# Transposes of the next element ahead of its loop turn, the last query tile in halves, row sums spread, and layer 1's values on VectorE

## The reference

```
layer 0:  deg = sum(adj, -1);  agg = adj @ x / max(deg, 1e-6);  relu(concat(x, agg) @ W.T)
layer 1:  Xw = X @ Wv + bv;  sj = Xw @ aw[:d];  si = Xw @ aw[d:]
          alpha = A * exp(leaky_relu(sj[None, :] + si[:, None] + ab, 0.2))
          T = alpha / (sum(alpha, -1) + 1e-12)
          H = sum_k (T^k X) @ Wk[k] + bk[k]   (k = 0, 1, 2);   relu(H)
layer 2:  three graph convolutions adj @ (x @ W) + b, relu after the first two
layer 3:  attention, 8 heads of 32: softmax(q k^T * scale * (adj + adj)) v, then @ Wo + bo
```

## Time and profile before

| | us |
|---|---|
| median of 3 runs (lowest, highest) | 3148.42 (3145.50, 3149.03) |
| the profiled execution | 3147.59 |
| its span, first to last instruction | 3145.7 |
| TensorE busy (matmul) | 3023.7 |
| VectorE busy | 2083.8 |
| ScalarE busy | 1724.0 |

### The profile page before, as it was taken

The page is one execution under the profiler, slowest core; times in us unless marked ns, Lnnn a source line. Parts: engine busy times, 40 slices in busy tenths (PEclk is TensorE's granted clock), DMA queues, the critical chain, the costliest instruction groups (busy, mean ns, idle before and its releaser), DMA issues.

```text
span 3145.7 us, 71077 instructions
## 1 busy us (share of the span) xinstructions
PE 3023.7 (96%) x28188; PEld 2644.0 (84%) x28188; DVE 2083.8 (66%) x4020; ACT 1724.0 (55%) x3048; POOL 453.5 (14%) x1666
## 2 busy tenths in 40 slices
PE   6999999999999999999999999999999999999999
PEld 6988789887898778987789877898778987789877
DVE  5637976379762797627975289753887438874387
ACT  3525854258552684426844278542784327853377
POOL 0101211012110122101221012111121111211112
PEclk9999999999999999999999999999999999999999
DMA  5122131121321213202133021330213302133110
GB/s 218 36 72 69 45 145 54 57 70 45 142 77 37 66 52 135 90 28 66 49 135 108 11 72 42 135 108 14 68 51 125 108 14 72 50 124 108 28 39 19
DMA packets 145271, 234.50 MB, mean 75 GB/s; under 512 B 12840, under 2 KB 113965, under 8 KB 144941
## 3 DMA queue, kind: packets, MB, share of 16 engines
q1 hardware_dynamic: 144940, 229.96, 22.5%
HBM read 120.86 MB, written 83.89 MB: 65 GB/s over the span
## 4 chain that ended last, share of the span: by engine, by line
PE 80%; DVE 10%; ACT 3%; issue 2%; SPq 2%; POOL 2%; DMA 0%; DVEq 0%; POOLq 0%; ACTq 0%
PE ps L725 15%; PE ps L497 15%; PE ps L499 14%; PE ps L498 14%; PE ps L715 9%; PE ps L743 7%; DVE rsum L1280 2%; PE ps L598 2%; SPq L400 1%; PE ps L587 1%; PE ps L756 1%; DVE ev L1379 1%; PE ps L555 1%; DVE t_lo L1210 1%; POOL rstd L461 1%
## 5 line engine op out<-in xcount | busy, mean ns | idle before, releaser
L1466 DVE CUSTOM_DVE_ANT_0 r<-ps,adjn 128x1024 f32<-128x1024 f32 x512 | 620.7, 1212 | 19.5 <-DVE xr L1502 10.3
L1141 ACT ACTIVATE r<-r,nmax 128x1024 f32<-128x1024 f32 x512 | 584.9, 1142 | 23.0 <-POOL nmax L489 22.6
L497 PE MATMUL ps<-u_hi,t_hi 128*128 128x256 f32 x2048 | 589.9, 288 | 5.8 <-DVE u_lo L1190 4.8
L499 PE MATMUL ps<-u_hi,t_lo 128*128 128x256 f32 x2048 | 579.2, 283 | 0.0
L498 PE MATMUL ps<-u_lo,t_hi 128*128 128x256 f32 x2048 | 578.8, 283 | 0.0
L725 PEld LDWEIGHTS ps<-ident,r 128*128 128x128 f32 x4096 | 462.5, 141 | 115.4 <-issue 77.6
L725 PE MATMUL ps<-ident,r 128*128 128x128 f32 x4096 | 536.7, 274 | 7.3 <-DVE pt L1482 6.9
L1482 DVE COPY pt<-ps 128x512 f32<-128x512 f32 x512 | 352.9, 689 | 92.6 <-PE ps L725 75.0
L497 PEld LDWEIGHTS ps<-u_hi,t_hi 128*128 128x128 f32 x2048 | 391.2, 191 | 14.3 <-DVE t_lo L1190 7.7
L907 ACT ACTIVATE pt<-ps 128x512 f32<-128x512 f32 x512 | 304.0, 594 | 175.8 <-PE ps L725 161.9
L498 PEld LDWEIGHTS ps<-u_lo,t_hi 128*128 128x128 f32 x2048 | 391.1, 191 | 0.0
(11 more groups left out here) (162 smaller groups left out, 5233.9 us busy)
## 6 DMA issues: line engine op xcount, KB each, us to landing
adjn<-in_adj SPq DMA_DIRECT2D x64, 512.0 KB, 3.4
t_spill<-t_hi SPq DMA_DIRECT2D x64, 512.0 KB, 4.5
t_spill<-t_lo SPq DMA_DIRECT2D x64, 512.0 KB, 5.3
t_hi<-t_spill SPq DMA_DIRECT2D x32, 1024.0 KB, 5.3
t_lo<-t_spill SPq DMA_DIRECT2D x32, 1024.0 KB, 8.0
xn<-in_x SPq DMA_DIRECT2D x16, 512.0 KB, 4.5
x_spill<-xn SPq DMA_DIRECT2D x64, 128.0 KB, 1.7
q_stack<-u_hi SPq DMA_DIRECT2D x64, 128.0 KB, 2.4
```

Source lines behind the costliest of these rows:

```text
L497: pe.matmul(dst, a_hi, b_hi, start=first, stop=False, skip_group_check=check)
L499: return pe.matmul(dst, a_lo, b_hi, start=False, stop=last, skip_group_check=check)
L1141: act.activation(r[:, s % RSLOTS, :], r[:, s % RSLOTS, :], ACT.Exp, bias=nmax[:, s % 4:s % 4 + 1], accum_out=prow[:, qt % 2, h:h + 1]).the ...
L1466: dve.tensor_tensor_reduce(out=r[:, s % RSLOTS, :], in0=ps[:, 2 * (s % 2):2 * (s % 2) + 2, :].rearrange("p a c -> p (a c)"), in1=adjn[:, q ...
```

## The change

What it does, in the order of an element:

- **Drain.** For elements after the first, TensorE transposes the first halves of adj column blocks 0 and 1 at stage UNITS + 1 and of 2 and 3 at UNITS + 5, inside the previous element's loop; ScalarE and VectorE take them out there, and VectorE makes the first row sum there. For element 0 the four stand ahead of the loop. The order of units in layer 0 and of the g products is new (one g pair behind each adj block).
- **Last query tile.** The spread moves from stage UNITS + 4 to UNITS + 2, rbc ahead of tile 6's normalisation; the last context product goes to bank 0; c_f, c_hi, c_lo of this tile are made in two halves of 128 columns, and the output product takes them one by one.
- **Row sums.** One in the drain, three ahead of tile 0, four behind tiles 0 to 3.
- **Layer 1.** `s_j` half 0 is taken out by ScalarE (a copy with a bias), all four `v` pairs by `both_rows` on VectorE; v pair 0 goes ahead of the late transposes, pair 3 ahead of the first hop; the last three `s_i` move later, with a scratch output elsewhere.
- **Layer 1's row product.** Own parts are issued two tiles ahead.

The diff, cut to its core:

```diff
-    TP_L0 = adj_units(0, 1) + x_units(0, 0) + adj_units(2, 3) + x_units(0, 1) + adj_units(4, 5, 6, 7)
+    TP_L0 = ([("adj", j, half) for half in range(HALVES) for j in range(TPH)] + x_units(0, 0) + adj_units(4, 5) +
+             x_units(0, 1) + adj_units(6, 7))
...
-            return ((4, 5, 2, 3)[n % 4],)
+            return (2 + n % 4,)
...
-                [("sj", 0), ("v", 0), ("v", 1), ("sj", 1), ("v", 2), ("v", 3)] +
+                [("sj", 0), ("v", 0), ("v", 1), ("v", 2), ("sj", 1), ("v", 3)] +
...
+        def ctx_bank(grp):
+
+            return ACC if grp == 2 * NT - 1 else 6
...
             pe.wait_ge(set_act, 13)
+            for j in range(TPH):
+                transpose_adj(0, j, 0)
             for b in range(B):
 
-                transpose_adj(b, 0, 0)
-                transpose_adj(b, 0, 1)
+                for j in range(TPH):
+                    transpose_adj(b, j, 1)
                 transpose_x_half(b, 0, 0)
-                transpose_adj(b, 0, 2)
-                transpose_adj(b, 0, 3)
+                transpose_adj(b, 4, 0)
+                transpose_adj(b, 4, 1)
                 pe.wait_ge(drained, b + 1)
-                project_pairs(b, "g", W_L0G, xt_wait(b, 0), range(2))
+                project_pairs(b, "g", W_L0G, xt_wait(b, 0), range(1))
+                transpose_adj(b, 5, 0)
+                transpose_adj(b, 5, 1)
+                project_pairs(b, "g", W_L0G, xt_wait(b, 0), range(1, 2))
                 transpose_x_half(b, 0, 1)
-                transpose_adj(b, 0, 4)
-                transpose_adj(b, 0, 5)
-                project_pairs(b, "g", W_L0G, xt_wait(b, 0), range(2, PAIRS))
-                transpose_adj(b, 0, 6)
-                transpose_adj(b, 0, 7)
+                transpose_adj(b, 6, 0)
+                transpose_adj(b, 6, 1)
+                project_pairs(b, "g", W_L0G, xt_wait(b, 0), range(2, 3))
+                transpose_adj(b, 7, 0)
+                transpose_adj(b, 7, 1)
+                project_pairs(b, "g", W_L0G, xt_wait(b, 0), range(3, PAIRS))
...
                 s_j(b, 0)
+                project_pairs(b, "v", W_K2, xt_wait(b, 1), range(1))
                 transpose_x_late(b, 1, 1)
-                project_pairs(b, "v", W_K2, xt_wait(b, 1), range(1))
+                project_pairs(b, "v", W_K2, xt_wait(b, 1), range(1, 2))
                 transpose_x_late(b, 1, 2)
-                project_pairs(b, "v", W_K2, xt_wait(b, 1), range(1, 2))
+                project_pairs(b, "v", W_K2, xt_wait(b, 1), range(2, 3))
                 s_j(b, 1)
                 transpose_alpha(b, 0, 0)
-                project_pairs(b, "v", W_K2, xt_wait(b, 1), range(2, 3))
+                project_pairs(b, "v", W_K2, xt_wait(b, 1), range(3, 4))
...
-                project_pairs(b, "v", W_K2, xt_wait(b, 1), range(3, 4))
                 transpose_alpha(b, 1, 0)
...
+                own_part = lambda t: project(pr_bank(b, pr["h", t])[:, 0:F], W_K0, t).then_inc(pr_full, 1)
+                own_part(0)
+                own_part(1)
                 for t in range(NT):
-                    project(pr_bank(b, pr["h", t])[:, 0:F], W_K0, t).then_inc(pr_full, 1)
                     row_product(b, t, AF_P2)
+                    if t + 2 < NT:
+                        own_part(t + 2)
...
+                    if s in (UNITS + 1, UNITS + 5) and b + 1 < B:
+                        for j in ((0, 1) if s == UNITS + 1 else (2, 3)):
+                            transpose_adj(b + 1, j, 0)
+                    if s >= 12 and (s - 12) % H == 0 and (s - 12) // H < NT - 1:
                         spread_denominators(b, (s - 12) // H)
+                    if s == UNITS + 2:
+                        spread_denominators(b, NT - 1)
...
+                act.activation(sj_row[:, 0:512], ps[:, PR + pr["sj", 0] % 2, :], ACT.Identity,
+                               bias=e_const[:, 0:1]).then_inc(sj_act, 1)
                 x_late_transposed(b, 1, 1)
                 normalise(b, 0, NT - 1)
...
-                rows_from_pr(b, "v", range(2, 3))
...
-                rows_from_pr(b, "v", range(3, PAIRS))
...
+                    if s >= 21 and (s - 21) % H == 0 and (s - 21) // H < NT and s != UNITS + 5:
                         normalise(b, 3, (s - 21) // H)
+                    if s == UNITS + 8:
+                        normalise(b, 3, NT - 2)
...
+                    if s >= 13 and (s - 13) % H == 0 and (s - 13) // H < NT - 1 or s == UNITS + 3:
+                        qt = NT - 1 if s == UNITS + 3 else (s - 13) // H
...
+                            copy(c_hi[:, 0, :], c_f[:, 0, :]).then_inc(c_hi_ready, 1)
+                            act.wait_ge(c_raw, nth(b, NT + 1, NT + 1))
+                            copy(c_hi[:, 1, :], c_f[:, 1, :]).then_inc(c_hi_ready, 1)
+                    if s in (UNITS + 2, UNITS + 7) and b + 1 < B:
+                        adj_transposed(b + 1, (0, 1) if s == UNITS + 2 else (2, 3), (0,))
...
+                dve.wait_ge(xr_free, b + 1)
+                rows_from_pr(b, "g", U_G, range(3, PAIRS))
+                degree(b, range(1, TPH))
+                inverse_degrees(b, 0)
...
+                    if t < TPH:
+                        degree(b, (TPH + t,))
+                    if t == TPH - 1:
+                        inverse_degrees(b, 1)
+                        dve.wait_ge(deg_ready, nth(b, 3, 2))
+                    if 2 <= t < NT - 1:
                         s_i(b, t - 2)
...
-                s_j(0)
-                s_i(b, NT - 2)
+                both_rows(0)
                 x_late_transposed(b, 1, 1)
-                both_rows(0)
+                both_rows(1)
                 x_late_transposed(b, 1, 2)
                 weights(0, 0)
-                both_rows(1)
-                s_i(b, NT - 1)
+                both_rows(2)
                 weights(0, 1)
-                s_j(1)
+                s_j()
                 al_transposed(0, 0)
-                rows_from_pr(b, "v", U_V - 2, range(2, 3))
+                s_i(b, NT - 3)
+                both_rows(3)
                 weights(0, 2)
...
+                    if s == UNITS + 2 and b + 1 < B:
+                        adj_transposed(b + 1, (0, 1), (0,))
+                        degree(b + 1, (0,))
+                    if s == UNITS + 8 and b + 1 < B:
+                        adj_transposed(b + 1, (2,), (0,))
...
+                    if s == UNITS + 6:
+                        dve.wait_ge(rbc_ready, nth(b, NT, NT))
+                        for g in range(2):
+                            dve.wait_ge(ctx_done, nth(b, 2 * NT, 2 * NT - 1 + g))
+                            dve.tensor_tensor(c_f[:, g, :], ps[:, ctx_bank(2 * NT - 2 + g), g * P:(g + 1) * P], rbc[:, g, :],
+                                              ALU.mult).then_inc(c_raw, 1)
+                        for g in range(2):
+                            dve.wait_ge(c_hi_ready, nth(b, NT + 1, NT + g))
+                            rest(c_lo[:, g, :], c_f[:, g, :], c_hi[:, g, :], c_ready)
...
                         if qt == NT - 1:
                             dve.sem_inc(drained, 1)
+                            if b + 1 < B:
+                                adj_transposed(b + 1, (3,), (0,))
```

More of the change, by code:

```diff
@@ L134, in build_program @@
             t_lo = sb("t_lo", [P, NT, N], F32R, s)
+        with ExitStack() as s:
+            t_cols = sb("t_cols", [P, N - F], F32, s)
+            si_out = sb("si_out", [P, F], F32, s)
         with ExitStack() as s:
@@ L301, in tp_x, with adj_freed @@
             return tp["x", layer, half, 0]
[L303 to L305 removed]
+        def adj_freed(j):
+            return tp["adj", j, HALVES - 1] + 1
         def x_ready(layer, rows):
@@ L576, in transpose_x_late, with transpose_adj @@
                     last.then_inc(tp_full, 1)
[L578 to L589 removed]
+            def transpose_adj(b, j, half):
+                n = tp["adj", j, half]
+                tp_wait(b, n)
+                for t in range(TPH):
+                    i = TPH * half + t
+                    if j == 0:
+                        pe.wait_ge(adj_in[i], nth(b, 16, 16))
+                    last = pe.transpose(tp_bank(n)[:, t * P:(t + 1) * P], adjn[:, i, j * P:(j + 1) * P], ident)
+                last.then_inc(tp_full, 1)
             def transpose_alpha(b, part, t):
@@ L950, in x_late_transposed, with adj_transposed @@
                     copy(dst, src).then_inc(tp_hi, 1)
-            def adj_transposed(b, layer, j):
-                for half in range(HALVES):
-                    n = tp_a(layer, j) + half
-                    act.wait_ge(tp_full, nth(b, TP_UNITS, n + 1))
-                    copy(t_hi[:, j, half * 512:(half + 1) * 512], tp_bank(n)).then_inc(tp_hi, 1)
+            def adj_transposed(b, js, halves=range(HALVES)):
+                for j in js:
+                    for half in halves:
+                        n = tp["adj", j, half]
+                        act.wait_ge(tp_full, nth(b, TP_UNITS, n + 1))
```

(25 more changed lines are left out.)

128 lines of the change are left out of this document (58 added, 70 removed).

## The result

The changed kernel takes 3142.94 us (median of 20 runs, 3140.53 to 3144.97); the kernel before, on the same chip, 3148.88 us (20 runs, 3145.5 to 3150.87). The ratio is 0.9981, 95% interval 0.9974 to 0.9988: 5.9 us faster, where 10 were forecast. The profiled execution spans 3139.7 us (3145.7 before).

What follows compares the result with a forecast made beforehand. TensorE bounds the kernel (busy 3023.7 of 3145.7 us); only its idle and slow time can be won. Layer 1 and own products -10.4, drains +1.4, element 0 +0.3, tail -1.2: -9.9 us, 3138 us, range 3127 to 3149.

Steps and rivals of the forecast that it cites:

- The wait for ev: Layer 0, self product of tile 4: TensorE's 1.18 us wait behind eight row sums on VectorE goes.
- the long wait for weights: Layer 1, at 505.13: TensorE's wait of 1.63 us stays, since the order of its chain isn't touched.
- Layer 1: Reordered values and s_j, s_i in layer 1: -0.6 us per element, bounds -1.2 and +0.8.
- the wait of 0.8 us laid out at 491.0: Layer 1: TensorE waits 0.8 us for the third weights, which VectorE makes over a microsecond later than before.
- The own products: Layer 1's row product, at 530.52: a second own product fills the wait for u_lo, -0.7 us per element.
- element 0: First element, which has no drain ahead of it: +0.3 us.
- The tail: Behind the last element, no transposes in the drain: -1.2 us once, bounds -0.5 and -2.
- The price of the clock: Low clock behind the drain's idle stretches: about 1.1 us per drain, kept as before because the gap stays.
- +0.2 per drain: Net per drain: output 1.3 us later, row product 1.4 later, ev wait of 1.18 gone; bounds -1.0 and +1.2.
- the drains did not work: Rival: VectorE's steps overlap better or the clock stays up, drains give -1.0 us each, 3130 us; chance 0.2.
- the gain was not given back in layer 1: Rival: drains cost +0.7 us each and layer 1 gives nothing as VectorE bounds it, some 3146 us; chance 0.25.
- VectorE did not run a pair late there: Rival: in layer 1 VectorE runs a full pair late, delaying later weights, 3159 us, slower; chance 0.1.

Runs made afterwards that it cites:

- the part alone: Only the layer 1 part (v0 ahead of the late transposes, all value pairs on VectorE, first s_j on ScalarE) on the kernel before: 3140.49 us, 0.9974.
- the run with the row sum out of the drain: Changed kernel with ScalarE, VectorE and g product orders corrected, and all four first-half row sums ahead of tile 0: 3093.58 us, 0.9826.
- ScalarE's order, The run with ScalarE's order mended: Changed kernel with ScalarE's copies of the second halves of adj blocks 0 to 3 ahead of tile 7's normalisation: 3119.9 us, 0.9912.
- the four parts: Kernel before with own products ahead, row sums spread, layer 1 part and last query tile in halves, no transposes in the drain: 3112.67 us, 0.9891.
- the g order: Changed kernel with x's second half ahead of the second g pair, blocks 5 and 6 ahead of the third, block 7 last: 3126.51 us, 0.9929.
- VectorE's order: Changed kernel with tile 6's statistics ahead of the first two subtractions, the drain's row sum behind tile 7's statistics: 3133.22 us, 0.9953.
- the last run above: Kernel before with one edit, ScalarE taking out the next element's first four transposed blocks ahead of the last tile's normalisation: 3132.67 us, 0.9947.
- that run: Changed kernel with the ScalarE, VectorE and g product orders all corrected, the row sum still in the drain: 3106.5 us, 0.9866.

## Why the prediction was right, and where it was off

**The sign and the mechanism held.** In the first drain each step came where the queues had been laid out: the output product at 427.18 (forecast 427.1), the normalisation at 431.49 (431.3 to 431.4), the x transposes at 433.44 (433.3) after 3.18 us idle (3.4), the third g product after 0.86 us (0.95), the second self product after 0.79 (0.96), the row product at 449.67 (written as 449.5; the terms of the prediction, 433.3 + 16.66 - 1.9 + 0.95 + 0.96 - 0.3, give 449.67, and 1.65 where its sum took 1.4). c_f to output takes 1.01 us in halves against 1.39 in the earlier trace rows, 0.38 saved where 0.3 was taken. The wait for ev is gone and the long wait for weights is unchanged at 1.63, as forecast.

**Layer 1** gave more: 1.1 us (the part alone), not 0.6. The mis-sized term is VectorE's queue: the wait of 0.8 us laid out at 491.0 came at 491.00, but with 0.54, and nothing else ran late behind it. That is half of the difference; the other 0.2 us are not traced. The own products gave 0.7 where 0.7 stood (56.92 to about 56.22 in each element, with the rest of the change on it), and the first u_lo wait of 0.60 is gone. **The tail:** from the same transposes of the last query tile (3124.80, before 3129.28) to the last output product 8.53 us against 9.78, 1.25 where 1.2 stood.

**The size was off by 4 us**, 5.9 for 10, so that 3142.94 us lies just outside the "some 4 us" about 3138. That it is not further off is partly luck: layer 1's surplus (about 4 us in eight elements) and a dearer clock (about 5) stand against each other. The output products are the milestones:

| output product | before | after | shift | forecast |
|---|---|---|---|---|
| first drain | 425.80 | 427.18 | +1.4 | +0.3 |
| seventh drain | 2752.63 | 2748.92 | -3.7 | -6.3 |
| last | 3139.06 | 3133.33 | -5.7 | -9.9 |

(Forecast by its own steps: +0.3 in element 0, less 1.3, and +1.3 for the later output; then -0.6 - 0.7 + 0.2 per element; at the last the +1.3 falls away and the tail's 1.2 comes off.)

*Element 0* was mis-sized by 1.1. Its x transposes start 3.5 us later than before (46.85 for 43.32), since eight units have to be filled and taken out ahead of them, where it was four, and no drain hides any. TensorE and VectorE:

```profile
41.17 4.52 PE L595 MATMUL ps<-ident,adjn 128*128 128x128 f32 x32 [1.30 <-ACT wsi_row L931]
46.85 1.16 PE L564 MATMUL ps<-ident,xn 128*128 128x128 f32 x8 [1.16 <-DVE t_lo L1228]
```

```profile
44.89 1.21 DVE L1255 TENSOR_REDUCE rsum<-adjn 128x1 f32<-128x1024 f32 x1
46.02 2.47 DVE L1228 TENSOR_TENSOR t_lo<-ps,t_hi 128x512 fp32r<-128x512 f32 x4
```

The wait of 1.16 us is the first row sum, which stands on VectorE between the subtractions of the first and the second halves. In the run with the row sum out of the drain it has also left this place, and the wait is gone: there the x transposes start 4.55 us after the first adj transposes (41.48 to 46.03), here 5.68. The prediction's +0.3 for element 0 names no price for it. The thirty-two transposes take 4.52 us in both, not 3.8 at 0.48 a unit; that the copies of ScalarE and VectorE set the pace of four banks in turn is my reading, and no run tests it.

*The price of the clock* is the other term. The prediction kept it as it was in each drain, at the 1.1 us of the drain of the earlier trace rows. In three drains the low stretch lasted about twice as long. From the x transposes to the long alpha wait it is 71.6 to 71.8 us in the elements behind those three, 70.8 behind a short one, 70.34 behind none:

```profile
820.22 1.16 PE L564 MATMUL ps<-ident,xn 128*128 128x128 f32 x8 [3.18 <-DVE t_lo L1228]
...
890.56 1.09 PE L605 MATMUL ps<-ident,al_area 128*128 128x128 f32 x8 [1.63 <-DVE rsum L1371]
...
1205.78 1.94 PE L564 MATMUL ps<-ident,xn 128*128 128x128 f32 x8 [3.18 <-DVE t_lo L1228]
...
1277.41 1.09 PE L605 MATMUL ps<-ident,al_area 128*128 128x128 f32 x8 [1.63 <-DVE rsum L1371]
```

890.56 - 820.22 is 70.34, 1277.41 - 1205.78 is 71.63. Three times 0.9 is 2.7 us. And the kernel before had paid in five drains only: the same piece takes 73.3 to 73.8 us there, but 72.6 in the fifth and the seventh, where the low stretch fell into idle time ahead of it. The earlier trace rows is one of these two. Both are among the doubled ones now, which is another 2 us. Together that is more than what is missing, and it ate the surplus of layer 1 (seven times 0.5 us): in sum these seven pieces take 498.0 us where they took 513.1, 15.1 less, and the prediction's terms make it 16.2.

The rest is 1.5 us in element 0 up to its long alpha wait (117.14 us where it was 115.97, and 0.3 less was forecast), 0.3 between the output products and the x transposes, and 1.1 between the long alpha waits and the output products. In this last piece the attention stretches, from the first score product to the last transposes of the query tiles, take 0.9 us more than before in sum over the eight elements, which is within what they differ among themselves (141.5 to 143.1 us in either kernel), so no cause is claimed for it.

**What the prediction did not see** is how large the two opposed halves of its sum were. It wrote +0.2 per drain as a net. By its own prices the parts without the drain's rearrangement were worth some 30 us (10.4 for layer 1 and the own products, 9.4 for the ev wait, 9.9 for the output's wait), so the rearrangement stood in it as a loss of 20 us, and it measured 30. The text did not weigh it as a loss that could be had back. The runs put names on it: ScalarE's order 23 us (of which 17.6 could be had in the kernel before, and 19.8 on the four parts), the g order 16.4, VectorE's order 9.7.

The rule of the clock gate that the prediction took from the Trainium skill ("TensorE: Matmul & The Clock Gate", section "HAM oscillation — how this bites in real kernels"), a cold start each time an idle gap recurs, holds for the 3.18 us gap in six drains of seven. "Each time" is more than the runs bear out: behind 2.84 us in the run of the four parts the clock fell in three drains of seven, behind the output's 1.86 us in the last run above in two. The run with ScalarE's order mended shows the other side: five waits of 0.67 to 0.96 us in each drain, and the granted clock stays at 1.00.

The rivals: the drains did not work (in all seven the output product starts 6.6 us after the last transpose of the query tiles, where it was 5.3), the gain was not given back in layer 1, and VectorE did not run a pair late there (0.54 us of wait where the rival needed over 2).

## What to carry to other kernels

Before moving work into an idle stretch, ask what ends that stretch: here a copy that was ready stood behind one instruction in ScalarE's queue that waited for something else, and swapping the two was worth 17.6 us alone, three times the whole change. Where a change has several parts, write each part's gain and loss apart before netting them, and try each alone: four gained 35 us, the fifth hid 30 of it. A filler that costs nothing in a gap (the row sum) is on the chain once the gap is closed, so settle its place last. A price that is read in one turn of a loop need not hold in the others: look at all of them before multiplying.

## What the runs showed of the chip that I had not expected

- An idle stretch of TensorE can be paid twice. Taking 1.8 us net out of each of seven drains, 12.4 us in all, gave 23 us; by the traces 8.3 us of TensorE's busy time went too, and the granted clock stayed at its upper level with waits of up to 0.96 us left. With a wait of 1.80 us it fell to 0.63 (mean of the window shown), in all seven drains of that run; with one of 1.86 us it fell in two of seven.
- The same wait does not bring the same low stretch: 3.18 us stands ahead of all seven x transposes of the changed kernel's drains, and the low clock with it lasted over 6 us in three, about half as long in three, and was absent in one. With 2.84 us in each drain of the four parts it was absent in four. What decides between these is not shown.
- Halving an instruction does not halve its time: c_f takes 0.42 us for 256 columns, and two of 128 columns take 0.49 together. In a chain over three engines the halves still saved 0.38 us, since they overlap.
